# A vision tower block on one core: finishing the feed-forward tile by tile in sorted order

## The reference

```python
h = einsum('bhid,oi,od->bho', x, weighted_sum, weight)       # (4, 512, 256)
h = h + mamba_blocks(layernorm(h))                           # 4 times the same block
# feed-forward, on z = layernorm(h), eps 1e-5
logits = z @ W_router                                        # (2048, 4)
expert_idx = argmax(logits)
inter = gelu(z @ W1[expert_idx] + b1[expert_idx])            # 1024 wide
y = inter @ Wo + bo + z
y = (y - mean(y)) * rsqrt(var(y) + 1e-12) * gamma + beta
out = h + y
```

## Time and profile before

| | |
|---|---|
| median of 3 runs | 1898.66 us (1896.55 to 1900.65) |
| the profiled execution's own time | 1891.32 us |
| its span, first to last instruction | 1889.2 us |
| mean granted TensorE clock | 0.984 of full |
| PE busy | 1782.5 us (94%) |
| DVE, ACT, POOL busy | 1552.8, 1543.8, 1510.4 us |

### The profile page before, as it was taken

The page is one execution under the profiler, slowest core; times in us unless marked ns, Lnnn a source line. Parts: engine busy times, 40 slices in busy tenths (PEclk is TensorE's granted clock), DMA queues, the critical chain, the costliest instruction groups (busy, mean ns, idle before and its releaser), DMA issues.

```text
span 1889.2 us, 31478 instructions
## 1 busy us (share of the span) xinstructions
PE 1782.5 (94%) x11920; PEld 1415.4 (75%) x11920; DVE 1552.8 (82%) x1707; ACT 1543.8 (82%) x2579; POOL 1510.4 (80%) x874
## 2 busy tenths in 40 slices
PE   6989899999999999999999999999999988789993
PEld 3447687878787878787878787878788777789993
DVE  1368989898989898989898989898989989853243
ACT  0269999999999999999999999999999987832230
POOL 0029999999999999999999999999999987631422
PEclk9999999999999999999999999999999989899997
DMA  7211111121212121211111111111111211163641
GB/s 272 99 68 45 58 47 68 44 71 40 74 38 76 37 71 44 71 44 67 48 62 52 59 56 57 58 54 61 50 65 46 80 57 68 38 250 129 231 143 59
DMA packets 46392, 144.24 MB, mean 76 GB/s; under 512 B 7009, under 2 KB 18529, under 8 KB 42914
## 3 DMA queue, kind: packets, MB, share of 16 engines
q1 hardware_dynamic: 41538, 114.97, 17.5%
q0 software_dynamic: 4704, 27.27, 4.0%
HBM read 119.67 MB, written 22.54 MB: 75 GB/s over the span
## 4 chain that ended last, share of the span: by engine, by line
PE 41%; ACT 24%; POOL 20%; DVE 8%; issue 6%; DMA 1%; SPq 0%; POOLq 0%; DVEq 0%; ACTq 0%
POOL hid L524 13%; ACT hid L709 12%; ACT dub_t L724 9%; PE b_ps L1469 8%; PE y_all L1482 7%; DVE hid L1141 6%; PE bank_a L1601 4%; POOL dub_t L515 4%; PE bank_b L1337 3%; PE y_all L1222 3%; PE bank_a L1337 2%; POOL du L505 2%; PE b_ps L1585 2%; PE y_all L1585 2%; PE bank_a L1346 2%
## 5 line engine op out<-in xcount | busy, mean ns | idle before, releaser
L1141 DVE TENSOR_TENSOR_SCAN hid<-hid,b_ps 128x512 f32<-128x512 f32 x1024 | 1199.2, 1206 | 102.0 <-PE b_ps L1469 89.6
L524 POOL TENSOR_TENSOR hid<-hid,c_rep 128x1024 f32<-128x1024 f32 x506 | 1191.8, 2390 | 97.7 <-DVE hid L1141 97.4
L1469 PEld LDWEIGHTS b_ps<-ident,dub_t 128*128 128x128 f32 x4096 | 486.4, 142 | 300.2 <-issue 180.5
L1469 PE MATMUL b_ps<-ident,dub_t 128*128 128x128 f32 x4096 | 630.7, 277 | 42.7 <-DVE hid L1141 40.4
L709 ACT ACTIVATE hid<-delta,neg_a 128x512 f32<-128x512 f32 x1024 | 659.6, 714 | 0.2
L1482 PE MATMUL y_all<-ident,hid 128*128 128x128 f32 x4096 | 620.5, 275 | 0.0
L724 ACT ACTIVATE dub_t<-du_t,b_t 128x512 f32<-128x512 f32 x784 | 505.2, 714 | 30.0 <-PE b_ps L1469 29.6
L1482 PEld LDWEIGHTS y_all<-ident,hid 128*128 128x128 f32 x4096 | 484.1, 142 | 2.9 <-POOL hid L524 2.7
L515 POOL TENSOR_SCALAR dub_t<-du_t,b_t 128x512 f32<-128x512 f32 x240 | 162.4, 702 | 0.0
L934 DVE SCALAR_TENSOR_TENSOR u<-bank_b,conv_w_sb,u 128x511 f32<-128x511 f32 (+2 forms) x192 | 139.6, 727 | 0.7
L1316 PE MATMUL bank_b<-xn,w_in_sb 128*128 128x512 f32 x256 | 129.9, 603 | 5.4 <-DVE u L934 3.9
(11 more groups left out here) (211 smaller groups left out, 1593.7 us busy)
## 6 DMA issues: line engine op xcount, KB each, us to landing
c_rep<-bc_dram SPq DMA_DIRECT2D x128, 512.0 KB, 3.7
hid<-x_t SPq DMA_DIRECT2D x4, 2048.0 KB, 8.5
xt<-x_dram SPq DMA_DIRECT2D x15, 512.0 KB, 3.4
x_dram<-x_out SPq DMA_DIRECT2D x15, 512.0 KB, 2.9
z_dram<-du SPq DMA_DIRECT2D x2, 1408.0 KB, 19.2
y_dram<-hid SPq DMA_DIRECT2D x22, 128.0 KB, 2.1
h_dram<-hid SPq DMA_DIRECT2D x4, 512.0 KB, 4.3
x_dram<-hid SPq DMA_DIRECT2D x3, 512.0 KB, 2.7
```

The lines of the kernel that those rows point to most:

```text
L524: nc.gpsimd.tensor_tensor(part, part, c_rep[:, n % 2, s % GROUP, :].unsqueeze(1) .broadcast_to([P, HALF, SEQ]), ALU.mult).then_inc(hc_read ...
L1141: nc.vector.tensor_tensor_scan(hid[:, i % RING, d, :], hid[:, i % RING, d, :], b_ps[d % 2][:, :], 0.0, ALU.mult, ALU.add)\
L1469: last = nc.tensor.transpose(b_ps[d % 2][:, c * P:(c + 1) * P], dub_t[:, i % DUB, c, d * P:(d + 1) * P], ident[:, :])
```

## The change

The feed-forward result is no longer brought back to token order before the last LayerNorm. Beside z, POOL scatters the residual rows h to a table `h2_dram` and the tokens' numbers, 4 bytes each, to a table `id_dram`, by the same positions. SP loads z and h rows side by side, and the numbers. For each tile DVE adds the PSUM result and z + bo (`add_y`), takes the moments, centers and multiplies by gamma (`tile_moments`), and after the root adds h + beta (`tile_finish`); POOL adds bo and beta to the rows of a turn (`add_rows`), takes the root of each tile (`tail_root`, two small instructions), and scatters the finished rows to the output (`send_out`). Rows that hold no token get numbers above 2047 (`pad_id`), and go to rows of the output tensor that are cut off. `keep_y`, `store_y`, `fetch_y` and `store_out` are gone. A tile's PSUM result lies in one half bank for tiles 0 to 6, and after that in two banks by turns.

The start changes too: ACT starts the loads of `x_t[0]`, in two halves, and of `wd`; DVE makes the weight product in two halves; the zero rows, now for four tables, come behind the weights, and two transfers that fill `id_dram` stand ahead of `load_x(1)`.

The diff, cut to its core:

```diff
+O_RING = 8
+BANKED = 6
+LAY_T = 5
...
# SP
                     for d in range(TAPD):
                         sp.dma_start(ws[d::TAPD, :, :], ...).then_inc(tw_in, 16)
-                        sp.dma_start(wd[d::TAPD, :], ...).then_inc(tw_in, 16)
...
-                    load_tok(0)
                     load_tok(1)
-                    sp.wait_ge(zero_made, 1)
-                    for g in range(2):
-                        sp.dma_start(z_dram[g] ..., du[:, 0, 0:D] ...).then_inc(z_zeroed, 16)
...                     # w_in, w_x, w_dt, a_log, conv_b, b_dt, d_skip, conv_w
+                    sp.wait_ge(zero_made, 1)
+                    for g in range(2):
+                        sp.dma_start(z_dram[g] ..., du[:, 0, 0:D] ...).then_inc(z_zeroed, 16)
+                        sp.dma_start(h2_dram[g] ..., du[:, 0, 0:D] ...).then_inc(h2_zeroed, 16)
                     store_h(0)
                     load_tok(2)
...
+                    sp.wait_ge(ids_made, 2)
+                    for g in range(2):
+                        sp.dma_start(id_dram[g].rearrange("(j p) o -> p j o", p=P),
+                                     pad_id[:, g * TILES:(g + 1) * TILES].unsqueeze(2), ...).then_inc(id_set, 16)
...
-                    for p in range(3):
-                        store_y(p)
+                    load_h2(0)
+                    load_ids(0)
                     load_z(1)
-                    for p in range(3, 9):
-                        store_y(p)
-                    store_out(0)
...
+                    load_h2(1)
+                    load_ids(1)
# POOL
+                    def tail_root(t):
+                        r = t % TC
+                        pool.wait_ge(t_bn, 2 * (t + 1))
+                        nc.gpsimd.tensor_scalar(f_norm[:, 1, r:r + 1], moments[:, 1, r, 1:2], 1e-12, None, ALU.add).then_inc(t_ve_ready, 1)
+                        pool.wait_ge(t_ve_ready, t + 1)
+                        nc.gpsimd.tensor_tensor(f_norm[:, 1, r:r + 1], f_norm[:, 1, r:r + 1], half_power[:, 0:1], ALU.pow)\
+                            .then_inc(t_root_ready, 1)
+
+                    def add_rows(p):
+                        n, g, j = len(TURNS[p]), TURNS[p][0] // TILES, TURNS[p][0] % TILES
+                        pool.wait_ge(tile_done, p + 1)
+                        pool.wait_ge(h2_in[g], 3 * 16)
...
+                        nc.gpsimd.tensor_tensor(rows, rows, rows3[:, 0:2, :] ..., ALU.add).then_inc(rows_added, 1)
+
+                    def send_h2(g, c):      # scatters one f_h2 row block to h2_dram[g] at pos
...
+                    def send_id(g, c):      # scatters 128 token numbers (4 bytes each) to id_dram[g] at pos
...
+                    def send_out(t):
+                        pool.wait_ge(res_ready, t + 1)
+                        if t % TILES == 0:
+                            pool.wait_ge(id_in[t // TILES], 16)
+                        nc.gpsimd.indirect_dma_start(out=out, out_offset=...(ap=row_id[:, t:t + 1], axis=0),
+                                                     in_=o_row[:, t % O_RING, :], in_offset=None).then_inc(o_out[t % O_RING], 16)
...
-                    fetch_y(2)
-                    fetch_y(3)
-                    tail_root(2)
-                    tail_root(3)
+                    for c in range(CH):
+                        send_h2(0, c)
+                    load_w1(3)
+                    load_w1(4)
+                    for c in range(CH):
+                        send_id(0, c)
+                    add_rows(0)
+                    for t in range(ALL_TILES):
+                        if t + WBUF < ALL_TILES:
+                            load_w1(t + WBUF)
+                        if t in (turn[0] for turn in TURNS) and TURN_OF[t] + 1 < len(TURNS):
+                            add_rows(TURN_OF[t] + 1)
+                        if t == 1:
+                            head_root(2)
+                            head_root(3)
+                        if t == LAY_T:
+                            for c in range(CH):
+                                send_z(1, c)
+                        elif t == LAY_T + 1:
+                            tail_root(t - 2)
+                            tail_root(t - 1)
+                            send_out(t - 3)
+                            send_out(t - 2)
+                        else:
+                            if t >= 1:
+                                tail_root(t - 1)
+                            if t >= 2:
+                                send_out(t - 2)
+                        if t == LAY_T + 2:
+                            for c in range(CH):
+                                send_h2(1, c)
+                        if t == LAY_T + 3:
+                            for c in range(CH):
+                                send_id(1, c)
+                    send_out(ALL_TILES - 2)
+                    tail_root(ALL_TILES - 1)
+                    send_out(ALL_TILES - 1)
# ACT, first instructions
+                    act.dma_start(hid[:, 0, :, :], x_t[0, :, 0:NI, :]).then_inc(x_first, 16)
+                    for d in range(TAPD):
+                        act.dma_start(wd[d::TAPD, :], w_t[d, :].partition_broadcast(P // TAPD)).then_inc(tw_in, 16)
+                    act.dma_start(hid[:, 1, :, :], x_t[0, :, NI:2 * NI, :]).then_inc(xT_in[0], 16)
# DVE
+                    for half in range(2):   # the weight product in two halves of 128x1024
...
+                    def add_y(t):
+                        dve.wait_ge(out_done, t + 1)
+                        dve.wait_ge(rows_added, TURN_OF[t] + 1)
...
+                        if t >= O_RING:
+                            dve.wait_ge(o_out[t % O_RING], 16 * (t // O_RING))
+                        tt(o_row[:, t % O_RING, :], out_ps(t), z_rows(t)[:, 0:D], ALU.add).then_inc(y_added, 1)
+
+                    def tile_moments(t):    # bn_stats, bn_aggr, then (row - mean) * gamma -> centered
...
+                    def tile_finish(t):
+                        r, o = t % TC, t % O_RING
+                        dve.wait_ge(t_root_ready, t + 1)
+                        dve.wait_ge(centered, t + 1)
+                        nc.vector.scalar_tensor_tensor(o_row[:, o, :], o_row[:, o, :], f_norm[:, 1, r:r + 1], z_rows(t)[:, D:2 * D],
+                                                       ALU.mult, ALU.add).then_inc(res_ready, 1)
...
                     for t in range(ALL_TILES):
+                        if t >= 1:
+                            add_y(t - 1)
                         if t in (turn[0] for turn in TURNS) and TURN_OF[t] + 1 < len(TURNS):
                             tile_copy(TURN_OF[t] + 1)
...
+                        else:
+                            if t >= 1:
+                                tile_moments(t - 1)
+                            if t >= 2:
+                                tile_finish(t - 2)
+                    last = ALL_TILES - 1
+                    tile_finish(last - 1)
+                    add_y(last)
+                    tile_moments(last)
+                    tile_finish(last)
# PE, project_out(t)
+                        elif t <= BANKED:
+                            pe.wait_ge(y_added, t)
                         else:
-                            pe.wait_ge(y_kept, TURN_OF[t])
+                            pe.wait_ge(y_added, t - 1)
# the output
-    out = nc.dram_tensor("out", (BATCH, P, TC, D), ...)
+    out = nc.dram_tensor("out", (BATCH * SEQ + ALL_TILES * P, D), ...)
...
+    return np.ascontiguousarray(got[0:BATCH * SEQ]).reshape(BATCH, SEQ, D)
```

285 lines of the change are left out of this document (129 added, 156 removed).

## The result

| | median, us | ratio to before, 95% interval |
|---|---|---|
| before, 7 runs | 1898.66 (1896.55 to 1901.73) | |
| changed, 7 runs | 1905.06 (1903.42 to 1905.95) | 1.0035 (1.0025 to 1.0045) |
| forecast | 1877.5 (1868 to 1889) | 0.989 |

The changed kernel is slower, where 0.95 stood on faster. Its profiled span is 1904.2 us. So of the 15.0 us between the two spans only about 6.5 are the change's by the ratio, and experiments are compared by their ratios or by stretches of their own traces.

What follows compares the result with a forecast made beforehand. No single engine bounds the 16 steps; TensorE bounds the feed-forward, and 29.1 us of tail follow. Start -5.5, tail -22.2 and feed-forward +6.5 sum to -21.2 us: 1877.5 us, range 1868 to 1889.

Steps and rivals of the forecast that it cites:

- The fills: Step 1, two id_dram fills ahead of load_x(1): taken to delay the program by 0 us, bounds 0 and +4.
- Rival 3: Slower: the id_dram fills hold up step 1; a loss of 3.8 us from 16 us a fill on; chance 0.04.
- d: Time of each id_dram fill; load_x(1) would be 2d later, of which 6.5 us are free.
- Start: First product: split x_t[0] loads and earlier wd let PE start at 9.4 us, -5.5 us, bounds -2 and -7.
- The second step: Start, zero rows ahead of load_tok(2): the token product hides them with 6 us to spare.
- Tail: After PE's end: 29.1 us shrink to 6.9, bounds 5 and 10, so -22.2 us.
- Feed-forward: +6.5 us: PE waits for POOL's lag, net +7.3, less 0.75 for keep_y; bounds 0 and +17.
- forecast wait for the copy before expert(11): Feed-forward: PE waits 8.5 us for the copy of tiles 11 and 12, behind POOL's root of tile 7.
- no other gap of over 1 us: Sign of a right forecast: apart from the wait before expert(11), PE has no gap over 1 us.
- Rivals 1: Feed-forward: POOL keeps up through cheap small operations and shorter sends, PE never stops; 1870 us, chance 0.18.
- rival 2: Feed-forward: half of 22 sends take 0.8 us more, PE waits 17 us; 1887 us, chance 0.20.
- Rival 4: The start gains nothing: split input lands no earlier, or load_tok(2) comes late behind the zeros; 1883 us, chance 0.06.

Runs made afterwards that it cites:

- before_fills: The kernel before plus only the two fills of id_dram in 4-byte pieces ahead of load_x(1): 1902.33 us, ratio to before 1.0055.
- fill_rows: The changed kernel with the id_dram fills written from a tile with 128 numbers side by side, 512 B a piece: 1892.48 us, ratio to before 0.9960.
- best4: Changed kernel with 512 B fills and id rows, z and h joined for batches 2 and 3, load_tok(1) held until ws, wd and half x_t land: 1869.65 us, 0.9886.
- wd_first: fill_rows with the four wd loads issued ahead of the first half of x_t on ACT's queue: 1895.25 us, ratio to before 0.9970.
- best2: As best4, but the second half of x_t is also held back until ws, wd and the first half have landed: 1885.36 us, ratio to before 0.9930.
- fill_rows_2: fill_rows repeated word for word in another group, on another chip: 1885.37 us, ratio to before 0.9969.

## Why the prediction was wrong

**The fills: the step that failed.** I took 0 with bounds 0 and +4, "nearer to the second since these have 5.6 KB each", from the bytes, though the count of pieces was what I had written down. Rival 3, at 0.04, came: `load_x(1)` was 18 us late, so d was about 9. That is below the 16 at which I had put a loss, but for a gain of 21.2 that was 14 too large itself. The price of the late load was not "2d less 6.5 free" = 11.6 alone, but about that plus the slow clock (3.58 us against 1.84) less what later slack gave back: 10.4 us in before_fills, about 14 by the ratios of the changed kernel and fill_rows. The Trainium skill (DMA: Bandwidth & Descriptors, Rules for kernel authors) had said one descriptor for each element; the trace agrees, with 3359 packets under 512 B between 76 and 102 us for 2816 elements. And the upper bound of +4 rested on a misreading: the 10.37 us of the earlier trace rows are the time that SyncE took to issue the two zeroings. To land, they took a median of 19.2 us, by a row of the page before:

```profile
z_dram<-du SPq DMA_DIRECT2D x2, 1408.0 KB, 19.2
```

By that row the load behind would have been some 13 us late (19.2 less 6.5), an estimate; an ordinary load was no bound at all.

**Start: -1.5 instead of -5.5.** DVE's product started at 12.10, not 8.2. The estimate carried a delay of 4.05 us over from a queue in which nothing large stood ahead of `wd`. Now ws, wd and both halves of `x_t` (3.1 MB) share the engines at 360 to 430 GB/s from 4 us on; that alone is about 8 us behind the first issue at 0.8 to 2 us, and their ends fall together. In best4, where nothing else was under way, DVE's product still started at 12.06. The Trainium skill (DMA: Bandwidth & Descriptors, Rules for kernel authors) says it: loads spread over several queues run on the same 16 engines and interleave. wd_first (15.88) and best2 (10.60) agree. I had listed these megabytes, for `load_tok(2)`, and not used them for the first product. The second step, that no zeros hold up `load_tok(2)`, held: no wait of PE at batch 2.

**Tail: -16.7 instead of -22.2.** The work itself was nearly right: from PE's end to the end of GpSimd's last send 4.6 us, with the root 0.25 + 0.57 and not 0.3 + 1.04. What failed is "from the last landing to the end of the span 0.5". GpSimd's end takes 7.8 us here. Before, POOL's last root ended at 1882.2, 7.0 us ahead of the end, but VectorE's finish and the last store lay behind it and set the end: SyncE waited 0.2 us on the barrier. So nothing in the profile before had this price in the open, and by the slope of the tail's table the change's 38 added indirect transfers made up about 3 us of it, an estimate.

**Feed-forward: +13.7 without the gaps, +22.5 in the profiled run, instead of +6.5.** The forecast wait for the copy before expert(11) was there, with its releaser and in its place: 5.8 us in the changed kernel (7.0 in fill_rows_2), forecast 8.5; GpSimd took 35.5 us from its first send of z (1767.0) to the root of tile 7 (1802.5), forecast 37.5, the difference being the cheaper roots (0.9 to 1.0 us each, forecast 1.5). Three terms were missing: the slow clock behind a wait (2.2 to 2.9 us here), the late h2 loads before `project_out(1)` (4.7 + 1.8 us), and the gaps (9.4 us net, on some chips; in the changed kernel's own trace they hid the wait for the h2 loads). In fill_rows_2 the terms are 6.5 + (7.0 - 0.9) + 2.2 - 0.8 for `keep_y` = 14.0, against 13.7 measured. I had said "no other gap of over 1 us", and had looked for what the added transfers do to POOL's queue, not to their neighbours.

**Rivals 1, 2 and 4.** POOL did not keep up. Most sends of the critical stretch took 0.96 us and none over 1.3, so rival 2 did not come; only beside the last of the scan, at 1668 to 1688 us, every other one took 1.8 to 2.0, as in the earlier trace rows. Rival 4 came nearly in full (1.5 of 5.5 us).

**The sum.** Without 4-byte fills it is -4.2 (the start, and 2.5 us more that I can't assign and that lie within the 5.5 us by which this start differs between traces) + 13.7 - 16.7 = -7.2 us, the 1882.1 of fill_rows_2 against 1889.2. The change was worth a third of what I said even where it gained, and two fills of 5.6 KB, which compute nothing, turned it.

## What to carry to other kernels

Price a transfer by its pieces and by its direction, and by a row of landing and not of issue; then by what it stands in front of: a table of numbers that nobody waits for can hold up a load that all wait for. Where a change adds transfers, look at what lands beside them, since a new neighbour costs even where its own queue has slack. And before moving work behind TensorE's end to GpSimd, look how long the program needs to close that engine, and count its indirect transfers.

## What the hardware showed

- 2816 pieces of 4 B from SyncE took 17.1 us to land at full DMA engines and 25 GB/s, 6 ns for each piece over all 16 engines. The same words in 22 rows of 512 B were gone from the path, and a load of 1408 pieces of 4 B from that table landed in 2.3 us, or 12.9 beside W1 loads, which it left at 379 GB/s.
- Eight indirect sends of 128 pieces landed in a median 10.2 us with 4 B, 5.5 us with 512 B. Loads beside them: 18.7, 11.3, and 9.5 us with no such sends.
- GpSimd's end took 6.5 to 7.9 us behind its last instruction where SyncE then waited on the barrier, in order of the indirect transfers of the program: 7.8 with 92, 7.5 with 88, 7.1 to 7.2 with 84, 6.5 with 76.
- Behind a wait the granted clock was at its lower level, 0.5 of full speed, for all or part of the next instructions: 3.58 us against 1.84 for 16 matmuls after 8.1 us, 5.41 against 3.62 after 4.7 and also after 2.7, 5.93 and 6.43 against 3.73 for 32 after 7.0 and 5.8. The price of a wait is its length and 1.7 to 2.9 us.
- Small instructions of GpSimd: a 128x1 addition 0.21 to 0.54 us, a 128x1 power 0.57 to 0.67.
